# Values behind the second maxima in each attention unit of a macaron transformer block

## The reference

```python
x = x + 0.5 * ffn(layernorm(x))      # 8 experts, top 2, capacity 1.25, hidden 512, gelu
x = x + attn(layernorm(x))           # 16 heads of 8, causal
x = x + 0.5 * ffn(layernorm(x))

# attn, for each batch and head
scores = where(causal, q @ k.T / 8 ** 0.5, -inf)
ctx = softmax(scores) @ v            # then ctx @ wo.T + bo
```

## Time and profile before

| | us |
|---|---|
| median of 3 runs (lowest to highest) | 1035.97 (1031.82 to 1037.62) |
| the profiled execution | 1038.4 |
| its span, first to last instruction | 1036.6 |
| TensorE matmuls busy | 831.8 (80%) |
| VectorE busy | 601.5 (58%) |
| ScalarE busy | 523.4 (50%) |
| GpSimd busy | 489.6 (47%) |
| mean granted TensorE clock | 0.89 of full |

### The profile page before, as it was taken

One profiled execution on the slowest core, in us unless ns is written; L12 is line 12 of the kernel. 1 busy time (PEld: TensorE's weight loads), 2 busy tenths in 40 slices (PEclk: granted clock), 3 DMA queues, 4 the chain that ended last, 5 costly groups with the idle time before them and its releaser, 6 DMA issues. The chain is left out here.

```text
span 1036.6 us, 18080 instructions
## 1 busy us (share of the span) xinstructions
PE 831.8 (80%) x6599; PEld 446.5 (43%) x6599; DVE 601.5 (58%) x1237; ACT 523.4 (50%) x841; POOL 489.6 (47%) x686
## 2 busy tenths in 40 slices
PE   8569999944668988888978899878887618999990
PEld 7437878742212223332333323323232316787770
DVE  7931211124767788888787977878775423334235
ACT  6323343442237776777556786566766303433330
POOL 5047455325652662646467522562224651545453
PEclk9769999986657999999799999999899758999995
DMA  7115575621451262341524224323202124423236
GB/s 204 73 26 153 148 217 145 192 63 51 130 162 66 53 189 48 89 144 43 174 76 105 99 53 152 85 65 106 53 18 79 53 63 149 130 79 97 78 136 228
DMA packets 96185, 110.81 MB, mean 107 GB/s; under 512 B 12279, under 2 KB 68763, under 8 KB 96104
## 3 DMA queue, kind: packets, MB, share of 16 engines
q1 hardware_dynamic: 84752, 88.86, 29.1%
q0 software_dynamic: 9216, 17.98, 6.8%
q10 hardware_dynamic: 2136, 2.91, 0.8%
HBM read 57.86 MB, written 52.89 MB: 107 GB/s over the span
## 5 line engine op out<-in xcount | busy, mean ns | idle before, releaser
L1903 DVE TENSOR_REDUCE m_blk<-banks 128x8 f32<-128x1024 f32 (+1 forms) x320 | 348.5, 1114 | 79.7 <-PE banks L1505 67.1
L1823 ACT ACTIVATE pt<-banks 128x1024 f32<-128x1024 f32 (+3 forms) x384 | 300.4, 811 | 145.1 <-PE banks L1489 142.7
L1537 PE MATMUL banks<-pt,vs 128*32 128x512 f32 (+3 forms) x1536 | 176.6, 534 | 7.2 <-POOL pt L2252 3.8
L1489 PE MATMUL banks<-qb,kp 64*128 64x512 bf16 (+3 forms) x768 | 132.6, 351 | 53.7 <-DVE m_blk L1903 45.2
L2252 POOL TENSOR_SCALAR_AFFINE_SELECT pt<-pt 128x512 f32<-128x512 f32 x128 | 81.6, 637 | 192.1 <-ACT pt L1823 191.7
L1505 PE MATMUL banks<-kp,qa 64*128 64x128 bf16 (+4 forms) x1152 | 126.4, 294 | 19.6 <-ACT pt L1823 11.6
L849 POOL DMA_INDIRECT xe<-xn_rows,slot_tok x80 | 79.9, 999 | 94.4 <-PE banks L1190 37.2
L675 POOL DMA_INDIRECT y_tab<-ys,ids x70 | 68.0, 972 | 81.5 <-DVE ys L635 64.5
L1106 ACT ACTIVATE he<-banks,b_up 128x512 f32<-128x512 f32 (+1 forms) x96 | 57.9, 616 | 89.9 <-PE banks L1190 89.5
L1505 PEld LDWEIGHTS banks<-kp,qa 48*128 48x128 bf16 (+1 forms) x1152 | 46.2, 99 | 130.3 <-ACT pt L1823 92.7
L585 ACT ACTIVATE hT<-banks,bfc 128x512 f32<-128x512 f32 (+1 forms) x96 | 56.3, 615 | 84.9 <-DVE bfc L607 48.8
(11 more groups left out here) (344 smaller groups left out, 1128.8 us busy)
## 6 DMA issues: line engine op xcount, KB each, us to landing
bucket<-zero SPq DMA_DIRECT2D x16, 660.0 KB
qb<-q_stack SPq DMA_DIRECT2D x32, 192.0 KB, 3.5
qa<-q_stack SPq DMA_DIRECT2D x30, 192.0 KB, 3.3
kp<-k_stack SPq DMA_DIRECT2D x30, 192.0 KB, 4.2
q_stack<-qp SPq DMA_DIRECT2D x18, 256.0 KB
k_stack<-kq SPq DMA_DIRECT2D x18, 256.0 KB
y_slots<-ye SPq DMA_DIRECT2D x16, 256.0 KB, 2.5
mid<-x SPq DMA_DIRECT2D x8, 512.0 KB, 3.6
```

The source lines that it names most:

```text
L1489: i = nc.tensor.matmul(ring[SLOT["score", 2 * u + pair]][:, s, 0:w], kp[g][rows_s, pair, kb * P:(kb + 1) * P], qb[par][rows_s, pair, q0:q0 ...
L1537: i = nc.tensor.matmul(o_bank[VW * h:VW * h + VW, q:q + w], vs[par][:, kb, h, :], pt[u % PTS][:, h, 0:w], start=u in (0, SECOND), stop=u i ...
L1823: nc.scalar.activation(pt[u % PTS][:, 2 * pair:2 * pair + 2, 0:w], ring[SLOT["score", 2 * u + pair]][:, :, 0:w], ACT.Exp, scale=SCALE).the ...
L1903: nc.vector.tensor_reduce(dst, ring[slot][:, :, 0:blocks * P].rearrange("p s (j k) -> p s j k", k=P), AX.X, ALU.max).then_inc(m_done, 1)
```

## The change

In a unit with two maxima TensorE's order becomes S, M, S', M', values, task. In units with one maximum (2, 3) or none (11), and in the last step, the order is unchanged. The other engines' programs, the ring and all semaphore values stay as they are.

```diff
                         for pair in range(2):
                             slot_free(("score", 2 * u + pair), n, more, first)
                             score(par, g, n, u, pair)
+                            if more and m0 + pair < m1:
+                                slot_free(("max", m0 + pair), n, more, first)
+                                maxima(ng, nb, m0 + pair, SLOT["max", m0 + pair])
                             if pair == 1:
                                 if u >= LAG:
                                     values(par, n, u - LAG)
                                 elif not first:
                                     values(1 - par, n - 1, NU - LAG + u)
-                            if more and m0 + pair < m1:
-                                slot_free(("max", m0 + pair), n, more, first)
-                                maxima(ng, nb, m0 + pair, SLOT["max", m0 + pair])
                             if is_last(b, g) and (u, pair) == (8, 0):
                                 out_task({"o_p0": at["l_p0"]}, "o_p0", b)
```

## The result

The change makes the kernel slower: 1060.41 us median (1054.76 to 1062.78, 4 runs) against 1036.8 (1031.82 to 1039.86, 4 runs), a ratio of 1.0242 with a 95% interval of 1.0194 to 1.0289. The same kernel timed once more with more runs gave 1058.79 against 1034.94, 1.0243 (1.0206 to 1.0281). The forecast was 1058, out of a sum of +23 us; measured were +23.6 and +23.9.

A forecast was written before the change was run, and what follows sets the result against it. In attention no engine is full; scores and maxima share three PSUM slots, scores waiting mostly for VectorE's reductions. Terms 4.2 + 5.4 + 12.6 + 0 + 0 + 1 = +23 us gave 1059 from the median; forecast 1058, range 1043 to 1077.

The forecast's parts named there:

- The loop: Full task-free units in attention: values stand in the loop through VectorE's reduction; 3.03 us a unit before, 2.86 after.
- units 0 to 2, one step: First units of each attention step: unit 0 +0.57, units 1 and 2 -0.27; together +0.3 a step, +4.2 us in all.
- no tasks (group 2, batch 0): Units 4 to 10 without tasks: 18.89 before, 18.88 after; short values lose what long ones gain.
- group 0, batch 2: Group 0 step with output tasks: tasks come on top of stretched units; 20.04 becomes 21.8, +1.8 in each of three steps.
- group 1, batch 2: Group 1 step with projections, ScalarE splitting them before the score: 22.01 becomes 26.2, +4.2 in each of three steps.
- group 2, batch 2: Group 2 step with the router: units 4 to 6 lose 1.5, VectorE's earlier chain returns it; 0, between -1 and +1 each.
- first step: First attention step, largely at the lower clock, an exponential late by 0.45 rather than 0.8: +1 us.
- the other nine: Attention steps outside the output-task and projection terms: router and group 3 taken as 0, first step +1, plus first units.
- lower bound of +8: Attention: three kinds of stretch taken at 0 give 1 us a step (9 less), and projections cost half.
- Faster: Rival: reductions were the bound in attention, so taking values out of that loop saves some 15 us, 1021; chance 0.08.
- No change: Rival: gains in full units pay for losses in task units, VectorE setting the pace; 1036, up to 1041; chance 0.10.
- The clock: Rival: regular TensorE waits bring 1.2 GHz; one full unit in each of 15 steps 1072, two 1085; chance 0.14.

The follow-up runs named there:

- late_rest: Kernel before, with the values put behind the second maxima only in units 4 to 10 without a task: 1026.28 us against 1035.85, ratio 0.9896.

## Why the prediction was right

**The loop and its replacement.** The step on which all else rests, that M' would wait for its own unit's exponential until 1.54 after S, came out as 1.57, against the earlier trace rows. That the values and the task would follow it rather than hide in it is read in the first unit and in the projection unit above, and the halved exponentials show that this wait is the price: shorten it by 0.42 and the new order is the better one.

**The terms.** Beside each other, expected and measured (profile of the changed kernel, units 4 to 10 where nothing else is said):

| term | before | expected | measured |
|---|---|---|---|
| units 0 to 2, one step | 6.78 | 7.1 | 7.07 |
| no tasks (group 2, batch 0) | 18.89 | 18.88 | 18.77 |
| group 0, batch 2 | 20.04 | 21.8 | 21.60 |
| group 1, batch 2 | 22.01 | 26.2 | 26.04 |
| group 2, batch 2 | 23.37 | 23.4 | 23.20 |
| first step, whole | 40.61 | 41.6 | 39.37 |

The term that was wrong is the first step, +1 expected and -1.2 measured (-0.8 in the second trace): unit 7 took 3.11 in place of 4.33, as it was not at the lower clock. It is small, and so is a slip in the first unit, whose terms add up to 2.59 and not 2.58. The three group 1 steps, foreseen as +12.6 in units 4 to 10 and measured as +12.1, are half of the loss.

**Where the sum had luck.** Whole steps, first unit and all, in the two traces of the changed kernel against the one of before (expected: the terms of the sum, with 0.3 a step for the first units):

| steps | expected | first trace | second trace |
|---|---|---|---|
| group 0 with output tasks, three | +6.3 | +6.2 | +7.5 |
| group 1 with projections, three | +13.5 | +13.2 | +12.4 |
| the other nine | +3.4 | +4.1 | -4.2 |
| sum | +23.2 | +23.4 | +15.6 |

The terms that rest on the mechanism came out in both. The other nine steps did not: in the first trace a router step grew by 4.4 us with the lower clock, while the task-free step of group 1, batch 3, shrank by 2.2. Its first unit went from 3.74 to 2.95 in both traces, which the sum did not have. That the first trace meets the sum within 0.3 us is thus partly luck. What bears the forecast out are the medians of ten runs, +23.6 and +23.9.

**Bounds.** The lower bound of +8 supposed that VectorE's other work would catch up. It did mainly where I had said so, in the router's units 7 and 8, and in the first unit just named.

**The rivals.** *Faster* had the right observation, that the move empties the wait for reductions (45.2 to 4.2 us), and fell over what it named itself: the exponential is not done when M' comes up. Where no task stands behind, however, the move made alone is good, as late_rest shows (0.9869 to 0.9923); I had priced it at nothing. In the whole change those units do measure nothing in a step without tasks (18.89 to 18.77). *No change* fell with the task units. *The clock*: in 784 to 808 us of the changed kernel it did take part. The stretch by engine (the column before the last two is the granted clock), and values in it:

```profile
792.00:800.00 8.00, 7.04 (x32) 1.19 (x32) 7.06 (x17) 3.51 (x4) 0.00 (x0) 0.50 0.01 2
...
797.44 1.93 PE L1537 MATMUL banks<-pt,vs 128*32 128x512 f32 x8
```

That step took 38.21 us (33.84 before). It is not a steady part of the change: the second trace of the same kernel has 34.27 for this step, and attention's time at 1.2 GHz, worked out as above, is 72 us before and 82 and 59 in the two traces after. The granted clock in attention, a sign that I had named, went from 0.93 to 0.92 in one and 0.94 in the other. The Trainium skill, TensorE: Matmul & The Clock Gate, "A second HAM failure mode", would have the clock go to and fro when TensorE idles briefly between groups that cycle PSUM. By that rule the new order should spend more time at the lower clock. The traces agree that it can fall in such a stretch and not that it does so as a rule: units with a wait of 0.74 us each stayed at the full clock.

**The queue.** In the first unit TensorE idles 0.80 us, from 369.00, with values queued whose exponentials GpSimd's mask had finished at 366.2; they did not pass. The Trainium skill (same page, "Architectural detail") names only weight loads as pulled ahead, and the trace agrees.

## What to carry to other kernels

When a few PSUM tiles go round between one producer and two consumers, each piece of independent work in the producer's stream covers one consumer's latency and lengthens the loop through the other. Write down, for each place it could stand, which loop it is in and what it covers, with the tasks behind it as well: the waits may just change places, and what matters is how much work still fits inside the longer one. And decide place by place: the same move, each part made alone, cost 19 us in the units with tasks and saved some 10 in those without.

## What the runs showed of the hardware

The time that attention spent at 1.2 GHz scattered between 41 and 82 us over the profiled executions of these kernels, and between 59 and 82 for two traces of one kernel. Unit 7 of the last router step took 4.19 us in the trace where it ran at 1.2 GHz and 3.11 in the other. I did not find what makes the clock fall in one run and not in another.

The clock is not the whole of the scatter. The part ahead of attention, in which these kernels do not differ, ended anywhere from 282.2 to 290.2 us in the traces of those that do the whole work. And in the 27 timed runs of the kernel before that late_rest was compared with, the time (1030 to 1041 us) does not follow the run's mean granted clock: 1030.07 us at 0.906 and 1030.06 at 0.891, 1037.99 at 0.902 and 1040.65 at 0.888. How much of the 1055 to 1064 us of the changed kernel's single runs is the clock stays open.
